# A graph and attention layer on one core: the residual's x, bias and base enter the PSUM group through an identity product, and ScalarE copies the sum out

## What is computed

```python
edge_index = jnp.stack([src, dst])
xn = _layernorm(x, axis=-1)                       # x: 1250 x 1024, f32
x = x + gnn(xn, edge_index, rms_w, W_down, Wl, Wr, att, W_up) + mix(xn, Wq, bq, ..., Wo, bo)
x = x + ffn(_layernorm(x, axis=-1), gate_w, up_w, down_w, s_in, s_in_down)

def mix(x, ...):                                  # linear attention, no softmax
    q, k, v = x @ Wq.T + bq, x @ Wk.T + bk, x @ Wv.T + bv
    return (q @ k.T * SCALE) @ v @ Wo.T + bo

def gnn(x, ...):                                  # graph attention over 40000 edges + loops
    x = rms_norm(x) * rms_w @ W_down              # 1024 -> 256, 4 heads of 64
    ...                                           # softmax over the edges of each receiver
    return out @ W_up                             # 256 -> 1024

def ffn(x, ...):                                  # all three operands fake-quantized to NVFP4
    hidden = silu(q(x) @ q(gate_w).T) * (q(x) @ q(up_w).T)
    return q(hidden) @ q(down_w).T
```

## Time and profile before

| | us |
|---|---|
| median of three runs (lowest, highest) | 905.53 (905.32, 908.13) |
| the profiled execution, its own time | 904.46 |
| its span, first to last instruction | 902.3 |
| TensorE busy | 854.7 (95%) |
| VectorE busy | 810.3 (90%) |
| ScalarE busy | 550.5 (61%) |
| POOL busy | 496.6 (55%) |
| mean granted TensorE clock, share of full speed | 0.977 |

### The profile page before, as it was taken

The page is one execution under the profiler, slowest core; times in us unless marked ns, Lnnn a source line. Parts: engine busy times, 40 slices in busy tenths (PEclk is TensorE's granted clock), DMA queues, the critical chain, the costliest instruction groups (busy, mean ns, idle before and its releaser), DMA issues.

```text
span 902.3 us, 9485 instructions
## 1 busy us (share of the span) xinstructions
PE 854.7 (95%) x2744; PEld 419.3 (46%) x2754; DVE 810.3 (90%) x923; ACT 550.5 (61%) x1949; POOL 496.6 (55%) x529
## 2 busy tenths in 40 slices
PE   7999999999999999999999999999999995989855
PEld 6885455644444444444444444444444442434322
DVE  6999998689999999999999999999998269788894
ACT  3314123356667887879999898789899443244242
POOL 3400648578666767877777788877775231010011
PEclk8999999999999999999999999999999998999978
DMA  9331535553555333663335633339738592113235
GB/s 301 112 117 32 150 118 173 140 194 102 77 168 187 92 89 91 195 210 100 103 102 192 194 102 96 97 96 198 234 97 167 129 231 71 74 24 55 39 46 88
DMA packets 66161, 114.68 MB, mean 127 GB/s; under 512 B 29287, under 2 KB 36100, under 8 KB 66090
## 3 DMA queue, kind: packets, MB, share of 16 engines
q0 software_dynamic: 22288, 64.21, 30.0%
q1 hardware_dynamic: 43818, 49.85, 17.3%
HBM read 89.15 MB, written 17.17 MB: 118 GB/s over the span
## 4 chain that ended last, share of the span: by engine, by line
DVE 47%; PE 37%; issue 5%; POOL 4%; DMA 3%; ACT 3%; SPq 0%; ACTq 0%; DVEq 0%; POOLq 0%
PE acc L760 29%; DVE acc_sb L1511 8%; DVE z L1673 8%; DVE turned L1503 7%; DVE turned L1671 7%; POOL round_mem L550 3%; PE acc L949 2%; PE turned L973 2%; PE acc L916 2%; DVE round_mem L1269 1%; DMA big_b<-big_b 1%; DVE big_a L1471 1%; ACT round_mem L1144 1%; DMA big_b<-in_x 1%; DVE big_b L1660 1%
## 5 line engine op out<-in xcount | busy, mean ns | idle before, releaser
L550 POOL DMA_INDIRECT round_mem<-msg_table,idx x352 | 344.7, 979 | 99.4 <-issue 79.1
L1144 ACT ACTIVATE round_mem<-round_mem,pz 128x65 f32<-128x65 f32 x1408 | 354.4, 398 | 7.6 <-DVE acc_sb L1511 3.5
L760 PE MATMUL acc<-wslot,big_a 128*128 128x512 f32 x512 | 220.3, 592 | 0.0
L760 PEld LDWEIGHTS acc<-wslot,big_a 128*128 128x128 f32 x512 | 97.1, 190 | 121.5 <-issue 121.3
L1511 DVE TENSOR_REDUCE acc_sb<-round_mem 128x260 f32<-128x1820 f32 (+1 forms) x62 | 121.6, 1962 | 8.5 <-ACT round_mem L1144 5.1
L1134 ACT ACTIVATE pz<-z 128x7 f32<-128x7 f32 (+1 forms) x248 | 55.4, 296 | 95.2 <-DVE z L1678 95.0
L760 PE MATMUL acc<-wslot,big_b 128*128 128x512 f32 x256 | 110.0, 592 | 0.0
L760 PE MATMUL acc<-big_b,wslot 128*128 128x512 f32 x256 | 110.0, 592 | 0.0
L1503 DVE TENSOR_TENSOR turned<-round_mem,turned 128x1560 f32<-128x1560 f32 (+1 forms) x62 | 105.4, 1700 | 2.4 <-DMA round_mem<-msg_table,idx 0.3
L1673 DVE TENSOR_REDUCE z<-turned 128x24 f32<-128x1560 f32 (+1 forms) x62 | 105.1, 1696 | 2.1
L1671 DVE SCALAR_TENSOR_TENSOR turned<-turned,att_sb 128x1536 f32<-128x1536 f32 (+1 forms) x62 | 103.6, 1671 | 0.0
(11 more groups left out here) (233 smaller groups left out, 1019.7 us busy)
## 6 DMA issues: line engine op xcount, KB each, us to landing
big_b<-in_x SPq DMA_DIRECT2D x11, 512.0 KB, 8.4
round_mem<-msg_table,idx POOLq DMA_INDIRECT x352, 2.8
big_b<-big_b POOLq DMA_DIRECT2D x9, 512.0 KB, 10.0
out_x<-big_b SPq DMA_DIRECT2D x9, 512.0 KB, 3.6
out_x<-acc_sb POOLq DMA_DIRECT2D x9, 512.0 KB, 5.4
wslot<-in_wv_t SPq DMA_DIRECT2D x2, 2048.0 KB, 9.7
wslot<-in_wk_t SPq DMA_DIRECT2D x2, 2048.0 KB, 9.0
wslot<-in_wo_t SPq DMA_DIRECT2D x2, 2048.0 KB, 9.2
```

The source lines that it names most:

```text
L550: pool.indirect_dma_start(xg[g % 4][:, j, :], None, msg_table, bass.IndirectOffsetOnAxis(idx[:, c, j0 + j:j0 + j + 1], 0)).then_inc(xg_in[ ...
L760: mm = nc.tensor.matmul(o(acc[:, n % 4, :]), a, b, start=first, stop=last)
L1144: ins = nc.scalar.activation(to[:, :, j], xg[g % 4][:, j, h * HR + 1:(h + 1) * HR], ACT.Copy, scale=pz[:, g % 2, j, h:h + 1])
```

## The change

Before, VectorE's `residual` adds `base` to the bank. Now TensorE multiplies `base[:, c]` by the identity as the last product of the bank's group (line 928 of the new kernel), so the bank holds the whole sum, and ScalarE's new `residual` copies it back to `base` with its row sum. The wait for `bias_added[c]` (for chunk 9 for `x_added`) moves from VectorE to TensorE. On ScalarE the residuals take places of their own, each chunk's `deviation` stands ahead of the Silu of its loop instead of behind it, and the attention copies of chunks 2 and 3 stand behind the deviation of chunk 0. POOL adds the bias of chunks 5 and 7 ahead of x of chunk 6. `PRODUCTS_AT` goes from 166 to 170.8. `X2_PLAN` stays.

```diff
-PRODUCTS_AT, GROUP_STEP = 166, {"p0c": 2.0, "bias": 1.0}
+PRODUCTS_AT, GROUP_STEP = 170.8, {"p0c": 2.0, "bias": 1.0}
...
                 if k == -1:
+                    for c in (5, EARLY):
+                        add_bias(c)
+                for c in [*whole_at((k, 1)), *whole_at((k, 2))]:
+                    deviation_root(c)
+                if k == -1:
                     for c in range(6, EARLY):
                         add_x(c)
-                    for c in (5, *range(EARLY, C - 1), *range(6, EARLY)):
+                    for c in [c for c in (4, 8, 7, 6) if c not in (AHEAD, AHEAD + 1, EARLY)]:
                         add_bias(c)
...
                 for k in range(2):
-                    mm = nc.tensor.matmul(to, gnn_tr[:, k, c * NC:(c + 1) * NC], wup_sb[:, k, h * HALF:(h + 1) * HALF],
-                                          start=(c < EARLY and k == 0), stop=(k == 1))
-                mm.then_inc(x2_full, 1)
+                    nc.tensor.matmul(to, gnn_tr[:, k, c * NC:(c + 1) * NC], wup_sb[:, k, h * HALF:(h + 1) * HALF],
+                                     start=(c < EARLY and k == 0), stop=False)
+                if c < C - 1:
+                    pe.wait_ge(bias_added[c], 16)
+                else:
+                    pe.wait_ge(x_added[EARLY], 16)
+                nc.tensor.matmul(to, ident[:], base[:, c, h * HALF:(h + 1) * HALF], start=False, stop=True).then_inc(x2_full, 1)
...
+            def residual(c, h):
+
+                act.wait_ge(x2_full, x2_made.index((c, h)) + 1)
+                nc.scalar.activation(base[:, c, h * HALF:(h + 1) * HALF], x2_bank(c, h), ACT.Identity,
+                                     accum_out=less_mean[:, c:c + 1] if h == 0 else mean_var[:, c, 1:2]).then_inc(x2_taken, 1)
...
+            take_attention(0)
+            take_attention(1)
+            residual(0, 0)
+            residual(0, 1)
+            deviation(0)
+            take_attention(2)
+            take_attention(3)
+            residual(1, 1)
             take_attention(4)
             take_attention(5)
             normalize(0)
-            deviation(whole[1])
+            residual(1, 0)
+            deviation(1)
...
                 if 0 <= k + 1 < C:
                     turn_over(k + 1)
+                now = ((k, 1), (k, 2), (k + 1, 0)) if k >= 0 else ((0, 0),)
+                for when in now:
+                    for half in added_at(when):
+                        residual(*half)
...
-                for c in whole_at((k, 0)) if k >= 0 else []:
-                    deviation(c)
+                for when in now:
+                    for c in whole_at(when):
+                        deviation(c)
```

More of the change, by code:

```diff
@@ L1175, in turn_over @@
                 nc.scalar.copy(q_t[c % 2][:, :, 0:NC], tpb[:, 0, :].rearrange("p (k n) -> p k n", k=KB)[:, :, 0:NC]).then_inc(q_taken, 1)
-            for c in range(4):
-                take_attention(c)
-            whole = [c for when in ((-2, 0), (-1, 0), (-1, 1), (-1, 2)) for c in whole_at(when)]
-            deviation(whole[0])
+            assert x2_added[0:6] == [(0, 0), (0, 1), (1, 1), (1, 0), (2, 1), (2, 0)]
+            take_attention(0)
[6 more added lines that the diff above has]
+            residual(1, 1)
             take_attention(4)
@@ L1189, in _ @@
             take_attention(9)
-            for c in whole[2:]:
-                deviation(c)
+            residual(2, 1)
+            residual(2, 0)
+            deviation(2)
             for k in range(-1, C + 2):
@@ L1212, in _ @@
                     scale_down(k - 2)
-                for c in [*whole_at((k, 1)), *whole_at((k, 2))] if k >= 0 else []:
-                    deviation(c)
         @block.vector
```

21 lines of the change are left out of this document (removed).

## The result

The changed kernel takes **938.06 us** (median of 4 runs, 937.4 to 938.94) where the kernel before took 905.81 beside it: a ratio of **1.0345**, 95% interval 1.0327 to 1.0362. It is slower by 32 us. The forecast was 932.0 with a range of 915 to 944, so sign and range held and the centre was 6 us low. The two medians differ by 32.2 us, where the forecast had 27.5.

The account below looks back on a forecast made before the run. It took the tail as bound by a chain through POOL, then a TensorE, ScalarE and VectorE loop. Adding 20.4 up to the first full step and 7.1 after it to 904.46 gave 932.0 us, range 915 to 944.

Parts of the forecast that it names:

- Part 1: Constant 166 to 170.8: base groups wait for later copies out of PSUM, so the base products end 5.3 us later.
- Part 2: Identity products on TensorE: one more per half, 0.86 us each, 17.2 us for 20, free only where TensorE idles.
- 1.7 + 0.9 + 5.2 + 6.9: Identity costs in us: chunk 0's two halves, half (1,0), six later identities, then eight halves after the first full step.
- Part 3: TensorE waits 10.6 us for bias 5, landing at 742.0, plus 1.5 of clock; VectorE's first full step 20.4 later, base delay included.
- Part 4: Later tail, +7.1 us: eight identities +6.9, chunk 9's halves waiting for ScalarE copies +6.8, earlier deviations -6.6.
- rival (c): Clock lost at each new TensorE wait, 1.5 us each, and VectorE's 2.6 us not carried over: 940, up to 944; chance 0.15.
- The −6.6 of part 4: Later tail: deviations ahead of Silu take some 2.8 us off two of VectorE's waits and about 1.0 off a third.

Follow-up runs that it names:

- the other bank: Changed kernel with half (8,1) copied one loop earlier and half (9,1) in bank 1 instead of bank 0: 924.18 us, ratio 1.0200.
- the three edits together: Changed kernel with constant 166, bias of chunks 5 and 7 added ahead of the roots, and (9,1) in bank 1: 913.57 us, ratio 1.0072.
- the three edits without identities: Changed kernel with constant 166, bias 5 and 7 ahead of the roots, (9,1) in bank 1, and the 20 identity products left out: 904.49 us, ratio 0.9973.

## Why the prediction was right, and where it was not

- **Sign and mechanism of the front of the tail: right.** The waits at the base products, the standstill before (5,1), the DMA that ends it and the step at 772 stand where the prediction put them (772.0 forecast, 772.58 measured).
- **Part 1, +5.3: measured 4.5**, and 3.9 in the time of the kernel with the constant back. What sets it is when the copy of base group 1 lets TensorE go on: 27.7 us after the start of the base products, where the prediction's numbers give 28.7. The waits were 2.69 and 0.55 instead of 3.9 and 2.2. The 1.7 us of slower records between them cost next to nothing, as the second wait shrank by as much: with 2.67, full clock and 1.89 the kernel with the other bank needs 102.9 us for the stretch, this one 103.3.
- **Part 2, 0.86 each: right in size.** Without all 20 the kernel is 14 to 15 us faster, where the terms of the sum had 14.7 (1.7 + 0.9 + 5.2 + 6.9). The sum put eight behind the first full step; nine start there, and 6.0 us, seven times 0.86, showed between the first and the seventh step. ScalarE's copy was taken at 0.7 and is 0.69.
- **Part 3, standstill: 8.77 for 10.6**, as the first products of (5,1) ended 1.6 us later; the 2.4 us of the clock in front are in that. The landing was forecast at 742.0 and came at 741.70: the issue 0.9 later, the transfer 6.80 instead of 8. The half clock behind it was sized from the earlier trace rows at 1.5 and was 2.66 (1.06 and 1.60). That the stretch came within 0.9 us is in part these errors of both signs.
- **Part 4, +7.1: this is the step that was wrong; 13.3 measured.** The waits for chunk 9's halves were 3.41 and 4.05 for 3.8 and 3.0 forecast, so their sum, 7.5, was close to the 6.8. Missing was the clock behind them, 4.5 us, and what the stretch behind the seventh step grew by, 1.3 against the kernel before and 1.9 against that with the other bank. The other bank took away 13.9 us in one stroke. That is rival (c), which had put 1.5 us on each new wait and 0.15 on its chance. The prediction charged the lost clock for the long standstill and not for waits half as long, though it had named them as near to it. The trace of the kernel before had such a case, which the prediction did not use: (8,0) there took 8.78 us for 16 records, behind a wait of 2.27 us and two short turns.
```profile
798.04 0.62 PE L938 MATMUL turned<-identb,round_mem 128*128 128x128 bf16 x8 [2.27 <-DVE round_mem L1616]
...
798.72 8.78 PE L916 MATMUL acc<-big_a,xhat_t 128*128 128x512 f32 x16
```
- **The −6.6 of part 4: the size held, the reason is half shown.** Without identities the six steps are 6.33 us shorter than before (90.57 against 96.90). It needs the early deviations (97.46 without them), as the step said. But early deviations in the kernel before give nothing (97.27), so they also need something that came with them: the copies on ScalarE with VectorE's relief, or POOL's roots ahead of its add. Which of them was not tried. Nor was it separated how much of the 6.3 is clock: the two slow stretches of the kernel before, 8.61 and 8.78 us for 16 records, are not there in the kernel without identities (7.09 and 7.08), which lost 1.7 us at another place.
- **Prices that were taken as adding do not where one hides another:** with the rest mended, TensorE waited 4.25 us for bias 5 again, and the traces of the three edits together are 4.8 us above the sum.

In the loop the change about pays for itself: 6.3 gained, 6.0 for the identities, and with the waits mended 96.60 against 96.90. What it loses, it loses in front of the first full step and, as it stands, at chunk 9.

The Trainium skill, page "TensorE: Matmul & The Clock Gate", section "HAM oscillation — how this bites in real kernels", says that the products behind a wait of some 3 to 5 us for a transfer start at half clock. The trace agrees at the waits of 3.41, 4.05 and 8.77 us, the first two of which end by a ScalarE copy and not by a transfer; the wait of 7.08 us that the prediction cites was ended by VectorE. The trace differs at that of 2.69 us, which is shorter and lost the clock too. An estimate by that rule, with the prediction's 1.5 us at each of the three further waits of 3 us or more that it had forecast (3.9, 3.8 and 3.0), would have been 936.5.

The page "DMA: Bandwidth & Descriptors" of the Trainium skill, section "Anatomy of one DMA — SWDGE (gpsimd) path", gives an estimate of 3.2 us for an add of 512 KB. No add of the bias landed in under 4.6 us in the changed kernel, and the one that mattered took 6.80.

## What to carry to other kernels

When a wait moves from one engine to another, look at when the new engine comes to it and what stands behind it in its order: VectorE came to the bias of chunk 5 at 736.2 and lost 1.95 us, TensorE came to it at 733.0 and lost 8.8 and the clock of what followed, and issuing two adds earlier cured it. On TensorE, where it is the bound, count each new wait of some 3 us or more for itself and for slower products behind it, 1.6 to 2.9 us here, though behind one of 3.50 us there were none. Behind shorter waits the loss was anything from nothing to 1.7 us. And when work is moved for another engine's relief, ask first whether the loop waits for that engine: with the deviations late, the loop was no shorter without VectorE's 20 adds.

## What the runs showed of the hardware

- The length of a wait alone does not tell whether TensorE's clock is lost behind it. In nine of the kernels TensorE waits the same 2.27 us for the same ScalarE copy before the same f32 products. The four records behind it took 1.98 or 1.99 us in four kernels, 2.68, 2.90 and 3.58 in three, and 3.68 in two; first the changed kernel, then the three edits without identities:
```profile
778.16 1.99 PE L922 MATMUL turned<-wslot,xr_sb 128*128 128x512 f32 x4 [2.27 <-ACT big_b L1159]
```
```profile
762.15 3.68 PE L925 MATMUL turned<-wslot,xr_sb 128*128 128x512 f32 x4 [2.27 <-ACT big_b L1158]
```
- For 16 records that take 7.1 us at full clock: 7.10 behind 2.29 us and 7.11 behind 2.67, but 8.80 behind 2.69; 8.83 behind 2.55 (the kernel without identities), 8.66 behind 3.41, and behind 4.05 us 10.03 in the changed kernel and 8.83 in the one without identities. Behind a wait of 3.50 us for VectorE (in the kernel without identities and with late deviations) the 16 records took 7.09. The wait of 4.25 was followed by 1.52 and 3.23 us for 1.02 and 1.88, that of 1.84 by 1.12. In the changed kernel the two waits for chunk 9 lie in stretches of these granted clocks (third figure from the end of a row):
```profile
830.00:848.00 18.00, 14.12 (x51) 6.51 (x49) 15.52 (x24) 7.58 (x15) 0.88 (x1) 0.91 0.26 58
848.00:870.00 22.00, 17.90 (x57) 8.06 (x57) 13.80 (x21) 5.07 (x8) 1.46 (x2) 0.84 0.16 25
```
- The granted clock from 60 to 120 us varies between executions of the same products, from 0.92 to 0.97 over the fourteen kernels, and what follows came 1 to 5 us later with the lower ones. The early part of a trace is no place to read a change's effect.
- ScalarE's copy of 128x512 out of PSUM with a row sum takes 0.60 us and 0.20 for reading the sum, 0.69 from start to end, as long as VectorE's add with its sum.
